# Evacuating the Q and K projections of a macaron block: one 2048-column copy on ScalarE, or two 1024-column copies on ScalarE and VectorE

## What is computed

```python
x = x + 0.5 * ffn(layernorm(x))      # W_real, W_imag unfolded from two small factors
x = x + attn(layernorm(x))
x = x + 0.5 * ffn(layernorm(x))

# attn, H = 16 heads of D = 64, chunks of CS = 64 rows
q, k, v  = split(x @ W_qkv)                       # (H, chunks, 64, 64) each
attn     = softmax(mask(q @ k.T * D ** -0.5))     # inside a chunk
local    = attn @ v
cum_k, cum_v = exclusive cumsum over chunks of the chunk means of k, v
cross    = sigmoid(q . cum_k * D ** -0.5)
out      = (local + cross * cum_v * 0.5) @ W_out
```

## Time and profile before

| | |
|---|---|
| median of 3 runs | 922.39 us (922.02 to 922.54) |
| profiled execution, its own time | 922.1 us |
| its span on the slowest core (core 5) | 920.6 us |
| spans of the eight cores | 916.0 to 920.6 us |
| TensorE matmuls, busy | 501.5 us, 54% |
| VectorE, busy | 387.1 us, 42% |
| ScalarE, busy | 166.4 us, 18% |
| mean granted TensorE clock, core 5 | 0.792 |

### The profile page before, as it was taken

One profiled execution on the slowest core, in us unless ns is written; L12 is line 12 of the kernel. 1 busy time (PEld: TensorE's weight loads), 2 busy tenths in 40 slices (PEclk: granted clock), 3 DMA queues, 4 the chain that ended last, 5 costly groups with the idle time before them and its releaser, 6 DMA issues.

```text
span 920.6 us, 8977 instructions; the slowest of 8 cores (916.0 to 920.6 us)
## 1 busy us (share of the span) xinstructions
PE 501.5 (54%) x3240; PEld 247.7 (27%) x3240; DVE 387.1 (42%) x839; ACT 166.4 (18%) x137; POOL 22.9 (2%) x26
## 2 busy tenths in 40 slices
PE   0000099933725825725724724725725824995998
PEld 0000033311512512512512512512512512442333
DVE  0399875670242242242242242242242243777222
ACT  0000000000340241341341341340341240000000
POOL 3000000000000000000000000000000000000000
PEclk9999999976956856956956956856956855997999
DMA  8600187035030030120120210170000004505822
GB/s 228 184 0 0 21 162 69 1 74 109 4 32 0 2 34 1 10 26 1 14 22 1 20 16 0 12 116 0 1 0 1 1 1 80 103 1 105 215 115 115
DMA packets 98957, 43.63 MB, mean 47 GB/s; under 512 B 93441, under 2 KB 93569, under 8 KB 98914
## 3 DMA queue, kind: packets, MB, share of 16 engines
q1 hardware_dynamic: 72002, 33.57, 15.2%
q0 software_dynamic: 26912, 9.49, 9.6%
HBM read 26.78 MB, written 8.39 MB: 38 GB/s over the span
## 4 chain that ended last, share of the span: by engine, by line
PE 52%; DVE 16%; ACT 14%; issue 11%; DMA 4%; SPq 1%; POOL 1%; DVEq 1%; ACTq 0%; POOLq 0%
PE PS L408 15%; PE PB L434 6%; PE PW L325 5%; PE PW L326 5%; PE PS L325 5%; PE PS L326 5%; ACT ptm L558 4%; DVE att_tmp L645 3%; DMA ln_tm<-g2i 3%; DVE ln_tm L651 3%; ACT L558 3%; PE PB L629 2%; ACT L593 2%; PE PW L624 2%; DVE ln_tm L204 2%
## 5 line engine op out<-in xcount | busy, mean ns | idle before, releaser
L408 PE MATMUL PS<-ln_fm,wqkv_j 128*128 128x512 bf16 x512 | 142.2, 447 | 72.0 <-DMA ln_fm<-ln_tm 30.3
L450 DVE CAST vt<-PB 128x512 bf16<-128x512 f32 x32 | 22.2, 694 | 225.2 <-PE PB L434 225.2
L624 PE MATMUL PW<-vt,ptm 128*128 128x65 bf16 x128 | 28.9, 225 | 155.1 <-DVE ln_tm L651 119.5
L408 PEld LDWEIGHTS PS<-ln_fm,wqkv_j 128*128 128x128 bf16 x512 | 56.2, 112 | 155.8 <-issue 116.0
L317 PE MATMUL PW<-b,ones_s 1*128 1x512 bf16 x16 | 6.5, 409 | 124.4 <-DVE ln_tm L204 114.9
L558 ACT ACT_TABLE_LOAD x32 | 41.1, 1283 | 138.8 <-PE PS L540 83.0
L420 ACT ACT_TABLE_LOAD x16 | 20.5, 1283 | 251.9 <-PE PS L408 251.9
L624 PEld LDWEIGHTS PW<-vt,ptm 128*128 128x128 bf16 x128 | 13.4, 104 | 179.5 <-issue 172.0
L434 PE MATMUL PB<-wqkv_j,ln_fm 128*128 128x128 bf16 x1024 | 58.5, 219 | 0.0
L434 PEld LDWEIGHTS PB<-wqkv_j,ln_fm 128*128 128x128 bf16 x1024 | 57.8, 98 | 1.9
L198 ACT ACT_TABLE_LOAD x3 | 3.8, 1283 | 267.4 <-DVE mv L192 158.9
(11 more groups left out here) (94 smaller groups left out, 739.5 us busy)
## 6 DMA issues: line engine op xcount, KB each, us to landing
x_tm<-x_in SPq DMA_DIRECT2D x4, 2048.0 KB, 29.2
y_out<-x_tm SPq DMA_DIRECT2D x16, 512.0 KB
wqkv_j<-w_qkv POOLq DMA_DIRECT2D x8, 768.0 KB, 8.9
wout_sb<-w_out POOLq DMA_DIRECT2D x1, 2048.0 KB, 16.7
ln_fm<-ln_tm SPq DMA_TRANSPOSE x64, 3.3
gm_s<-gm POOLq DMA_DIRECT2D x1, 256.0 KB, 15.0
ln_tm<-g1r POOLq DMA_DIRECT2D x1, 256.0 KB, 21.4
ln_tm<-g1i POOLq DMA_DIRECT2D x1, 256.0 KB, 22.0
```

The costliest lines, as they stand in the source:

```text
L408: mm = te.matmul(ps[:, half * 512:half * 512 + 512], wqkv_j[:, slot, part, f, :], ln_fm[:, f * T + tq * 512: f * T + (tq + 1) * 512], star ...
L450: s_dve.inc(v.tensor_copy(dst, ps[:].rearrange("p (b h d) -> p b h d", h=2, d=64)))
L624: te.matmul(pv[:, 0:65], ptA, vt[:, p * 130:p * 130 + 65], start=True, stop=True)
```

## The change

`PS4` is split into two tensors, `PSQ` and `PW1`. The copy out of PSUM after pieces 1 and 3 becomes four copies in a head pair: `PSQ` is copied by ScalarE after pieces 0 and 2 (columns 0 to 1023 of `kf` or `qf`), `PW1` by VectorE after pieces 1 and 3 (columns 1024 to 2047). `qk_evac_marks` gets four entries, each with the engine that made it. Piece 2 waits for the copy of piece 0, piece 3 for that of piece 1. The readers of `kf` and `qf` wait for both engines where they need both halves: the reduction of `kf` (L478 before), the score groups (L540), and the gate (L582), whose first half needs ScalarE's copy and whose second half needs VectorE's.

```diff
-        PS4 = _st.enter_context(nc.psum_tensor("PS4", [128, 2048], F32))
...
-        PSQ = _PsumView(PS4, 0)
-        PW1 = _PsumView(PS4, 1024)
+        PW1 = _st.enter_context(nc.psum_tensor("PW1", [128, 1024], F32))
+        PSQ = _st.enter_context(nc.psum_tensor("PSQ", [128, 1024], F32))
...
                     if ii >= 2:
-                        te.wait_ge(s_act.h, qk_evac_marks[0])
+                        kind_, mk_ = qk_evac_marks[ii - 2]
+                        te.wait_ge(s_act.h if kind_ == "act" else s_dve.h, mk_)
...
-                if ii % 2 == 1:
+                if ii % 2 == 0:
                     @block.scalar
-                    def _(sc, part=part, pe_mark=pe_mark):
+                    def _(sc, ii=ii, part=part, pe_mark=pe_mark):
                         sc.wait_ge(s_pe.h, pe_mark)
                         dst = qf if part == 0 else kf
-                        s_act.inc(sc.copy(dst[:, 0:2048], PS4[:, 0:2048]))
-                    qk_evac_marks.append(s_act.n)
+                        s_act.inc(sc.copy(dst[:, 0:1024], PSQ[:]))
+                    qk_evac_marks.append(("act", s_act.n))
+                else:
+                    @block.vector
+                    def _(v, ii=ii, part=part, pe_mark=pe_mark):
+                        v.wait_ge(s_pe.h, pe_mark)
+                        dst = qf if part == 0 else kf
+                        s_dve.inc(v.tensor_copy(dst[:, 1024:2048], PW1[:]))
+                    qk_evac_marks.append(("dve", s_dve.n))
...
-                v.wait_ge(s_act.h, qk_evac_marks[0])
+                v.wait_ge(s_act.h, qk_evac_marks[0][1])
+                v.wait_ge(s_dve.h, qk_evac_marks[1][1])
...
                     if q <= 1:
-                        te.wait_ge(s_act.h, qk_evac_marks[1])
+                        te.wait_ge(s_act.h, qk_evac_marks[2][1])
+                        if q == 1:
+                            te.wait_ge(s_dve.h, qk_evac_marks[3][1])
...
-                        te.wait_ge(s_act.h, qk_evac_marks[1])
+                        kind_, mk_ = qk_evac_marks[2 + sbp]
+                        te.wait_ge(s_act.h if kind_ == "act" else s_dve.h, mk_)
```

## The result

The changed kernel takes 884.03 us (median; 881.74 to 884.88), the kernel before, in the same comparison, 922.42 us. The ratio is 0.9585, with a 95% interval of 0.9572 to 0.9599. The profiled execution took 883.49 us, with a span of 881.9 us on its slowest core, core 3.

A forecast was written before the change was run, and what follows sets the result against it. The prediction took a chain hopping between engines, with no engine busy throughout, to bound the kernel. Its terms, 28.4 + 13.7 - 4.0 = 38.1 us saved, gave 884.3 us against the median 922.39, range 876 to 891.

The forecast's parts named there:

- Term 1: TensorE's wait before piece 2 for ScalarE's copy of K goes, with lost overlap: 28.4 us saved.
- Term 2: The second fall of the clock to 0.50, in pieces 2 and 3 after the idle stretch, goes: 13.7 us saved.
- Term 3: The cold start of pieces 0 and 1 at clock 0.50 stays and gets longer: 4.0 us more than now.
- Term 4: The added copies on VectorE hide under idle time and V's start: they cost nothing.
- Rival 1: Only the wait goes; the clock's fall still hits piece 2, 3 or V: 894 to 898 us, chance 0.06.
- Rival 2: Piece 2 still waits because ScalarE's load and copy outlast a piece: 887.7 us, chance 0.03.
- Rivals 3 and 4: The long matmul stretch gets less clock: V at 0.50, 941 us, chance 0.02; a level between, 922.4 us, chance 0.01.

The follow-up runs named there:

- Run 1: The changed kernel with all four copies of a head pair on ScalarE, none on VectorE; 883.08 us, ratio 0.9581.
- Run 2: The kernel before, its wait before piece 2 kept but filled with 14 result-less matmuls of 512 columns; 910.42 us, ratio 0.9878.
- run 3: The changed kernel with piece 2 waiting for VectorE's copy of piece 1 too; 891.76 us, ratio 0.9669.
- run 10: The kernel before with 5 result-less matmuls after each of the last four pairs of row blocks in the outputs; 900.01 us, ratio 0.9747.
- runs 5 to 10: Result-less matmuls added in various TensorE waits of the changed kernel, in run 10 of the kernel before; 861.85 to 900.01 us.
- run 6: The changed kernel with result-less matmuls in every TensorE wait between V and the next head pair; 892.76 us, ratio 0.9659.

## Why the prediction was right

**Term 1** (28.4 us) held. No piece waits. ScalarE's copy took 1.01 us where I had taken 1.02 from the exponential's row, VectorE's 1.22 to 1.23 where I had 1.2 to 1.4. Run 1 shows that the time of the start is what counts, not the share of work. ScalarE's copy starts at 418.04, where the table load ends (416.75 + 1.28 = 418.03). The Trainium skill, "ScalarE: Activation LUTs", section "What ACT_TABLE_LOAD costs", adds 1380 ns of drain to a switch to a different set; by an estimate from that figure a load and a copy would take 3.67 us, more than a piece. The rows have no such gap behind the load, and run 1, which does a load and a copy in each piece, doesn't wait. This doesn't contradict the page. The prediction took the load ahead of K's copy for such a switch, but no row tells which set a load names, and run 1 has a load ahead of each of four equal copies in a row.

**Term 2** (13.7 us) held: pieces 1, 2 and 3 take 3.45 us from start to start in all eight head pairs. Run 2 shows that the idle stretch was the cause, and run 3 that one of 1.48 us brought no fall. What I had not seen is that the number belongs to this kernel's timing. In run 10 the same idle stretch brought 4.4 us of falls in place of 13.7, and in the kernel before j=0 already had none.

**Term 3** (4.0 us given back) came out at 3.1. The excess of the eight head pairs is 18.4 us, 2.30 each, against 2.41 predicted and 1.91 before. The run of four low values did not come back, and the sum is not fixed: runs 1, 2 and 3 have 18.0, 19.5 and 14.4 us. That it is the distance of the head pairs that decides, as the prediction has it, fits this but is not shown, since no run changes the distance alone. To take 2.41 for all eight was a guess within wide bounds, and that it came within 0.9 us of the sum is partly luck. The bounds, 1.31 and 2.95, held too: the eight values lie between 1.4 and 2.95.

**Term 4** (nothing) held. VectorE's added copies took 19.6 us of its time and delayed nothing: the first V copy starts 2.06 us after V, as before.

The sum was 38.1 us and 38.6 were measured between the profiled executions. That they agree so well is partly chance. The terms as they came out make 28.4 + 13.7 - 3.1 = 39.0, and the rest of the execution gave 0.5 us back (2.66 less, 0.86 and 2.29 more, above), which I had put at nothing and did not follow up.

**The rivals.** Rival 1 (the cold stretch moves) is ruled out by the 17.4 us at 1.00 and by run 2. Rival 2 (piece 2 still waits) did not happen. Rivals 3 and 4 (the longer stretch is granted less) did not either: the rows show 1.00, and no level between that and 0.50 that isn't a mixture. The limit of 13/16, once three cores of a die run dense matmuls, that the Trainium skill names in "TensorE: Matmul & The Clock Gate", "Part 1: The HAM clock gate", did not appear in the changed kernel on any of its eight cores. The 0.81 in runs 5 to 10 is that figure, on four cores at once, but for 4.9 to 6.3 us only and with 1.00 behind it while the matmuls go on.

## What to carry to other kernels

When one copy empties two PSUM buffers at once, both are out of use for its whole length. Split the copy so that each part runs while the other buffer is being filled; whether a second engine helps is a separate question, and here it didn't. An idle stretch of TensorE has a second price, paid after it in matmuls at half clock, but it depends on when the stretch comes (none to 2.86 us a head pair here, for the same 3.38 us of idleness). Where the trace before shows it, it can be read off and counted; for a kernel that is shifted in time, leave it open by the range of the head pairs. Result-less matmuls in TensorE's waits can buy that clock back (865.6 and 861.9 us against 884.0), provided that no matmul that is free to run, and for which another engine waits, stands behind them on the queue.

## What the runs showed that I had not expected

- Two more result-less matmuls in each of four waits decided whether the projections began at 0.50 or at 1.00 in the head pairs behind them, and with it 11 to 14 us (877.1 against 865.6, ratios 0.9518 and 0.9367).
- On the slowest core, an idle stretch of 3.38 us was followed by a fall in seven of eight head pairs of the kernel before and in three of eight of run 10. One of 1.48 us was followed by none in eight of eight.
- A higher mean clock is no gain by itself: 0.91 in run 6 came with 892.8 us, 0.79 in the changed kernel with 884.0.
- The records have a third level of the granted clock, 0.81, on four of the eight cores in six of the twelve profiled executions, for 4.9 to 6.3 us each.
